# A gather kernel: eight of 180 superblocks fetched row by row with plain transfers from SyncE and ScalarE

## The reference

```
h = jnp.maximum(_layernorm(x, axis=-1), 0.0)
xs = h[src]
for i in range(4):
    mask = (edge_type == i)[:, None]
    msgs = msgs + jnp.where(mask, xs @ W[i] + b[i], 0.0)
out = x + jax.ops.segment_sum(msgs, dst, num_segments=N)
```

## Time and profile before

| | |
|---|---|
| timed runs, median of 3 | 2638.77 us (2616.4 to 2645.23) |
| profiled execution, span from its first to its last instruction | 2029.2 us |
| instructions in the profile | 24251 |
| mean granted clock of TensorE | 0.758 |
| DMA, mean over the span | 71 GB/s |

### The profile page before, as it was taken

How to read it: one execution, slowest core, us unless ns; L and a number is a source line. 1 busy time by engine, 2 the same in 40 slices (tenths; PEclk the granted TensorE clock), 3 DMA queues, 4 the chain that set the end, 5 groups by cost and what they waited for, 6 DMA issues and landing times.

```text
span 2029.2 us, 24251 instructions
## 1 busy us (share of the span) xinstructions
PE 1116.0 (55%) x5394; PEld 930.4 (46%) x5395; DVE 714.7 (35%) x1589; ACT 169.6 (8%) x565; POOL 1536.1 (76%) x1575
## 2 busy tenths in 40 slices
PE   6952545456564554654646556456555555554555
PEld 2322444344454444544535455445544444444554
DVE  6862223132332332433424334243322222232333
ACT  4530011010010100101001001010000000000000
POOL 7777777777777777777777777777777777777775
PEclk9985767776665776767878767787777777787788
DMA  9962221212122112211212121211312222212222
GB/s 305 328 206 54 51 52 50 53 49 52 51 50 52 50 49 52 51 51 49 50 52 50 50 52 50 51 50 50 104 51 70 51 51 52 69 51 52 69 52 59
DMA packets 94959, 144.09 MB, mean 71 GB/s; under 512 B 27065, under 2 KB 57267, under 8 KB 94947
## 3 DMA queue, kind: packets, MB, share of 16 engines
q0 software_dynamic: 50016, 102.53, 19.8%
q1 hardware_dynamic: 40537, 39.02, 5.8%
q10 hardware_dynamic: 4394, 2.40, 0.4%
HBM read 111.76 MB, written 32.09 MB: 71 GB/s over the span
## 4 chain that ended last, share of the span: by engine, by line
POOL 70%; issue 24%; PE 3%; DMA 1%; POOLq 1%; DVE 0%; ACT 0%; DVEq 0%; ACTq 0%; PEldq 0%
POOL messages L338 65%; POOL early_x L330 6%; PE ps_sum L710 2%; DMA messages<-message_table,row_stage 1%; PE ps_y L737 1%; PE ps_y L728 0%; POOLq L342 0%; POOLq L344 0%; DMA src_rows<-in_src 0%; PE ps_sum L746 0%; POOLq L345 0%; DVE onehot L593 0%; POOLq L246 0%; ACT row_stage L407 0%; DVE acc L585 0%
## 5 line engine op out<-in xcount | busy, mean ns | idle before, releaser
L338 POOL DMA_INDIRECT messages<-message_table,row_stage x1443 | 1420.5, 984 | 439.7 <-issue 437.9
L710 PE MATMUL ps_sum<-messages,onehot 128*128 128x128 f32 x4438 | 843.4, 370 | 852.9 <-DMA messages<-message_table,row_stage 769.7
L710 PEld LDWEIGHTS ps_sum<-messages,onehot 128*128 128x128 f32 x4438 | 791.0, 277 | 904.5 <-issue 890.5
L593 DVE SCALAR_TENSOR_TENSOR onehot<-node_iota,tile_base,dst_col 128x512 f32<-128x512 f32 x586 | 431.1, 749 | 1234.2 <-PE ps_sum L710 1147.0
L407 ACT COPY row_stage<-table_row 128x8 int32 (+2 forms) x181 | 35.7, 198 | 1602.5 <-PEq L715 1597.8
L330 POOL DMA_INDIRECT early_x<-in_x,src_col x120 | 113.5, 946 | 41.6 <-issue 39.4
L665 PE MATMUL ps_y<-w_sb,h_t 128*128 128x512 f32 x196 | 104.7, 626 | 4.6 <-DVE y L524 4.3
L737 PE MATMUL ps_y<-y 128*128 128x512 f32 x240 | 106.8, 598 | 0.0
L603 DVE SCALAR_TENSOR_TENSOR y<-key_iota,tile_base,key_col 128x1024 f32<-128x1024 f32 x60 | 75.9, 1285 | 35.5 <-PE ps_y L737 35.5
L585 DVE TENSOR_TENSOR acc<-acc,ps_sum x294 | 82.1, 279 | 2.3 <-PE ps_sum L710 2.1
L524 DVE TENSOR_TENSOR y<-ps_y,bias 128x512 f32<-128x512 f32 x98 | 66.9, 684 | 16.5 <-PE ps_y L665 11.4
(11 more groups left out here) (63 smaller groups left out, 147.5 us busy)
## 6 DMA issues: line engine op xcount, KB each, us to landing
message_table<-y SPq DMA_DIRECT2D x98, 256.0 KB
messages<-message_table,row_stage POOLq DMA_INDIRECT x1443
out<-acc SPq DMA_DIRECT2D x6, 896.0 KB
acc<-in_x SPq DMA_DIRECT2D x4, 896.0 KB, 7.5
early_x<-in_x,src_col POOLq DMA_INDIRECT x120
acc<-in_x ACTq DMA_DIRECT2D x2, 896.0 KB, 10.3
acc<-in_x SPq DMA_DIRECT2D x1, 832.0 KB, 6.9
src_rows<-in_src SPq DMA_DIRECT2D x1, 640.0 KB
```

Of the source, the lines that this page charges most:

```text
L338: pool.indirect_dma_start(messages[:, k, t, :], None, table_rows, bass.IndirectOffsetOnAxis(ap=row_stage[:, k, t:t + 1], axis=0)).then_inc ...
L593: nc.vector.scalar_tensor_tensor(out=onehot[:, a:z, :], in0=node_iota[:, :].unsqueeze(1).broadcast_to([P, z - a, P]), scalar=tile_base[:, ...
L710: ins = nc.tensor.matmul(ps_sum[:, bass.ds(q % 2, 1), 0:d], onehot[:, t, :], messages[:, k, t, :], start=(t == 0), stop=(t == tiles - 1))
```

## The change

Eight superblocks (`ROW_SBS`) leave GpSimd's list. For each of them SyncE fetches the 128 rows of each of 5 edge tiles (`SP_TILES`) and ScalarE those of the other 3, with one plain transfer for each row. A superblock's row numbers are first copied into one partition (`load_row_list`), then read 16 at a time into registers, and each register gives the row of one transfer (`fetch_rows`). The rows land in `row_messages`, two superblocks large, which uses the room of the lists of types and destinations (`pair_rows`); so the fetches wait until the first stage is over. When all rows of one have landed, each of the two engines counts a semaphore up, and TensorE waits for both. Seven of the row superblocks come after five rounds each (two of two with an early superblock behind, and one), the eighth ahead of the last round. SyncE's output stores stand behind all its row fetches.

The row numbers in the untransposed list are kept by a second multiply-add on VectorE (`table_rows_kept`). GpSimd's gathers are written out without a loop and read `table_row` directly; `row_stage` is gone, and GpSimd waits for the free slot itself. ScalarE's copies of the early sums move to VectorE. The order of superblocks changes accordingly in all engines, and the numbers in `order` with it.

```diff
+ROW_SBS = 8
+SP_TILES = 5
-    rounds = (full_sbs - EARLY_SBS) // SLOTS
+    rounds = (full_sbs - EARLY_SBS - ROW_SBS) // SLOTS
+    mixes = ROW_SBS - 1
+    mix_early = 2
+    mix_rounds = 2 * EARLY_ROUNDS + 1
+    def load_row_list(eng, n, rows, a, z, signal):
+        first = row_sb_id(n) * SB_TILES
+        eng.dma_start(rows[:, :].rearrange("o (t e) -> o t e", e=P),
+                      src_rows[first % P + a:first % P + z, first // P, :]).then_inc(signal, 16)
+        eng.wait_ge(signal, (n + 1) * 16)
+
+    def fetch_rows(eng, n, rows, row_at, t, signal):
+        regs = [eng.alloc_register(f"{eng.engine.name}_row{r}_{nc.next_id()}") for r in range(16)]
+        for q in range(P // 16):
+            eng.reg_load(regs, rows[0:1, bass.ds(row_at + q * 16, 16)])
+            for r in range(16):
+                p = q * 16 + r
+                row = eng.snap(regs[r], min_val=0, max_val=node_tiles * P * n_types - 1)
+                eng.dma_start(flat_row_messages[p:p + 1, bass.ds((t + (n % 2) * SB_TILES) * d, d)],
+                              table_rows[bass.ds(row, 1), :]).then_inc(signal, 16)
...
+            for n in range(ROW_SBS):
+                load_row_list(sp, n, sp_rows, 0, SP_TILES, sp_rows_loaded)
+                if n >= 2:
+                    sp.wait_ge(row_sb_used, n - 1)
+                with sp.Fori(0, SP_TILES) as t:
+                    fetch_rows(sp, n, sp_rows, t * P, t, sp_row_landed[n])
+                sp.wait_ge(sp_row_landed[n], SP_TILES * P * 16)
+                sp.sem_inc(sp_rows_gathered, 1)
+
             sp.wait_ge(store_after_ready, 1)
...
-            with pool.Fori(0, rounds) as i:
+            for i in range(rounds):
                 for k in range(SLOTS):
-                    pool.wait_ge(stage_ready, i * SLOTS + (k + 1))
-                    pool.sem_inc(slots_taken, 1)
-                    gather(k, SB_TILES)
-            pool.wait_ge(stage_ready, rounds * SLOTS + 1)
-            gather(0, last_tiles)
+                    gather(i, k)
+            gather(rounds, 0, last_tiles)
...
+            for n in range(ROW_SBS):
+                load_row_list(act, n, act_rows, SP_TILES, SB_TILES, act_rows_loaded)
+                make_early_h(n * mix_early)
+                if n >= 2:
+                    act.wait_ge(row_sb_used, n - 1)
+                fetch_rows(act, n, act_rows, 0, SP_TILES, act_row_landed[n])
+                if n < mixes:
+                    make_early_h(n * mix_early + 1)
+                with act.Fori(1, SB_TILES - SP_TILES) as t:
+                    fetch_rows(act, n, act_rows, t * P, t + SP_TILES, act_row_landed[n])
+                act.wait_ge(act_row_landed[n], (SB_TILES - SP_TILES) * P * 16)
+                act.sem_inc(act_rows_gathered, 1)
...
+                        dve.wait_ge(h_sums_done, p + 1)
+                        nc.vector.tensor_copy(h_sums[:, :, :], ps_y[:, 0, :].rearrange("f (t n) -> f t n", n=P)).then_inc(h_sums_ready, 1)
+                        nc.vector.tensor_copy(edge_counts[:, :], ps_y[:, 1, 0:P]).then_inc(h_sums_ready, 1)
...
+                    if rows_of is None:
+                        pe.wait_ge(gathered[k], needed)
+                    else:
+                        pe.wait_ge(sp_rows_gathered, needed)
+                        pe.wait_ge(act_rows_gathered, needed)
...
+                r = mix_early * EARLY_ROUNDS
+                table_round(s + r * SLOTS, n * mix_rounds + r)
+                row_superblock(s + mix_rounds * SLOTS, n)
```

More of the change, by code:

```diff
@@ L186, in gnn_program @@
     early_gathered = sem("early_gathered")
+    table_rows_kept = sem("table_rows_kept")
+    sp_rows_loaded = sem("sp_rows_loaded")
+    act_rows_loaded = sem("act_rows_loaded")
+    sp_row_landed = [sem(f"sp_row_landed{n}") for n in range(ROW_SBS)]
+    act_row_landed = [sem(f"act_row_landed{n}") for n in range(ROW_SBS)]
+    sp_rows_gathered = sem("sp_rows_gathered")
+    act_rows_gathered = sem("act_rows_gathered")
+    row_sb_used = sem("row_sb_used")
     e_stats_taken = sem("e_stats_taken")
@@ L334, in _, with table_sb_id, gather @@
                 pool.wait_ge(y_stored[k], 16 * node_tiles // Y_SLOTS)
-            def gather(k, tiles):
+            def table_sb_id(i, k):
+                if i < mixes * mix_rounds:
+                    return EARLY_SBS + i // mix_rounds * mix_ids + i % mix_rounds * SLOTS + k
+                i -= mixes * mix_rounds
+                return end_id + i * SLOTS + k + (1 if i >= end_rounds - 1 else 0)
+            pool.wait_ge(index_cols, groups + 1)
+            def gather(i, k, tiles=SB_TILES):
+                pool.wait_ge(slot_free[k], i + 1)
+                at = table_sb_id(i, k) * SB_TILES
                 for t in range(tiles):
@@ L487, in index_to_f32 @@
                                                    in1=type_rows[:, two, :], op0=ALU.mult, op1=ALU.add).then_inc(index_f_ready, 1)
+                    nc.vector.scalar_tensor_tensor(out=src_rows[:, two, :], in0=src_rows[:, two, :], scalar=float(n_types),
+                                                   in1=type_rows[:, two, :], op0=ALU.mult, op1=ALU.add).then_inc(table_rows_kept, 1)
                 elif part == 1:
@@ L617, in superblock, with run_with_early @@
                     dve.free_register(r)
[L619 to L620 removed]
+            def run_with_early(s, i):
                 superblock(s, SB_TILES)
@@ L699, in _, with superblock @@
             p_reg, early_count = counter(pe, "early_pair")
-            def superblock(s, k, tiles, needed):
+            def superblock(s, k, tiles, needed, free, rows_of=None):
                 lo, hi, regs = load_range(pe, s)
```

133 lines of the change are left out of this document (74 added, 59 removed).

## The result

The changed kernel takes 5716.3 us (median of 4 runs, 5710.6 to 5724.8), the kernel before beside it 2627.6 us (4 runs, 2614.0 to 2645.2). The ratio is 2.187, 95% interval 2.176 to 2.198. The prediction had the sign right and the size wrong: 3826 us was forecast, and 5716 lies outside the range too.

What follows compares the result with a forecast made beforehand. GpSimd's gathers bound the kernel before; after the change SyncE's row fetches would: 141 start + 2570 rows + 420 loads + 52 lists and waits + 33 last stretch = 3216 us, plus 609.6 outside the span = 3826 us; range 2530 to 5200.

Steps and rivals of the forecast that it cites:

- The bound of the kernel before: GpSimd's rate of one 128-row gather in 1.289 us, with GpSimd busy 76% of the 2029.2 us span.
- 82.5 us for 64 gathers: On GpSimd, 8 of 180 full superblocks leave: 64 gathers at 1.289 us each removed.
- SyncE's start at 141 us: SyncE's row fetches can start at about 141 us, after the table is stored and the list has landed.
- the register load of sixteen: On SyncE, one load per 16 rows, taken at 1.14 us; 320 with fused instruction and gaps make 420 us.
- the last stretch: Behind SyncE's last row: 27 us of TensorE's remaining work and 6 us for sums and stores.
- the mechanism: TensorE waits for SyncE at eight row superblocks, about 174 us each, frees no slots, and GpSimd stops.
- the row, forecast at 0.502 us without its load: On SyncE, each row costs 0.090 fused instruction, 0.08 dispatch and 0.332 transfer issue; 5120 rows make 2570 us.
- The prediction's estimate of 0.427 us: One transfer instruction on SyncE by the skill's 512 cycles at 1.2 GHz; would make the sum 4312 us.
- outside the span and fixed: The 609.6 us between timed median and profiled span were taken as outside the span and added to the sum.
- Rival 2: The 609.6 us belong to the work, so late SyncE gives 3216 us, or 2603 at lowest prices; chance 0.2.
- The chance of 0.12 on a dearer row: Rival: SyncE's rows cost more, up to 0.926 us of issue and 6867 us in all; over 4700, chance 0.12.
- Rival 3: Rows are hidden and GpSimd stays the bound: faster, 2556 or 2531 us; chance 0.18.

Runs made afterwards that it cites:

- e11: Kernel before, with only GpSimd's gathers reading offsets straight from the table's row and ScalarE's copies gone: 2030.0 us beside 2027.4, ratio 1.001.
- e10: Changed kernel with no row fetched at all, TensorE multiplying what the buffers hold: 1942.0 us beside 2027.4, ratio 0.958.
- e12: Changed kernel with all rows fetched, but GpSimd making one of eight gathers in its own superblocks: 4668.1 us beside 2027.4, ratio 2.303.
- e2: Changed kernel with row fetches written out for each tile, so each destination is constant and each row one piece: 4059.3 us, ratio 1.569.
- e0: Kernel before with only the register values bounded that SyncE waits against before output stores: 2595.1 us beside 2594.7, ratio 0.997.
- e17: The kernel of e12 once more in another group of runs: 4665.9 us beside 2028.0, ratio 2.299.
- e3: Changed kernel with only 16 of each tile's 128 rows fetched: 2583.0 us, ratio 0.999 to the kernel before.
- e15: The kernel of e3 once more in another group of runs: 2622.6 us, ratio 1.000.
- e4: On top of e2, ScalarE's three tiles of each row superblock not fetched: 3909.8 us, ratio 1.499.

## Why the prediction was wrong in size

**What held.** The bound of the kernel before, in a short group; the written-out gathers and ScalarE's copies at nothing (e11); 82.5 us for 64 gathers (85.3 in e10); SyncE's start at 141 us in a short group (139.9); the register load of sixteen, taken at 1.14 and measured at 0.973; the last stretch, roughly (33 us forecast, 44 in e12, 4663.8 less 4619.5); and the mechanism: TensorE waits eight times for SyncE, GpSimd stops for want of slots, GpSimd's gathers no longer set the time. That each wait is 370 us (2964.8 / 8) and not 174 comes of the dearer row, stalls included.

**First failed step: the row, forecast at 0.502 us without its load.** In e12, which has no stalls, the mean time from start to start is 0.120 for the fused instruction (0.130 was forecast with its gap), 0.065 for the MOVE (not in the sum) and 0.600 for the transfer with its gap (0.372 was forecast). Together 0.785: 0.283 us more on 5120 rows, 1449 us. The loads with their fused instructions came out at 348 us instead of 420. The order of instructions shows one register instruction ahead of a transfer, and I counted one; in the trace there are two. The kernel before has such a MOVE as well, ahead of 70 of its 98 table stores:

```profile
L280 SPq MOVE message_table<-y x70: 29/29/38, 36.0 to 132.6; - x70
```

The transfer I took from the nearest likeness of its addresses (0.332, 98 table stores). The row that was nearest in the shape of its pieces, many small ones into one partition, was the 0.926. With the same addresses of the source and the same bytes, 16 pieces took 0.547 and one piece 0.225 (e2). One reading of the rows was wrong, without much weight: 1.835 and 1.642 are the longest loads of two registers, but the first ones took 0.729 and 0.786.

By these the sum for the span is 140 + 4019 + 348 + 113 + 44 = 4664 us, where 4019 are the rows (5120 x 0.785) and 113 is what is left of the time from 140 to 4619.5 (52 forecast). Of these 113 us 91 go by in the branches that close 39 passes of the loops over tiles, 2.3 us each; the prediction had no term for them. My sum was 3216.

The prediction's estimate of 0.427 us rests on the 512 cycles that the Trainium skill, DMA: Bandwidth & Descriptors, gives for such an instruction on previous generations. No row here agrees: 0.225 for a whole row, 0.332 for a table store, 0.547 for a row in 16 pieces. The traces have no single figure per transfer; between the row in one piece and the row in 16 it differs by more than two.

**Second failed step: "outside the span and fixed".** A span was 1.8 to 2.3 us under its own execution's time in every run here. The 609.6 us were the difference between two kinds of executions: 107 us in the table stage and 462 in waits for slots, in e0. Rival 2 had them in the work, which is right. But it then let the late SyncE hide them, which is wrong: in the long groups SyncE is delayed too. Its rows start 130 us later (270 instead of 140) and lose 5120 x (1.055 - 0.875) = 922 us to stalls. 130 + 922 = 1052, and 5716.3 less the 4667 of e12 and e17 is 1049. Those two stand for the changed kernel in a short group, where it was not run itself.

**So the ledger** from 3826 to 5716: take the 609.6 out (3216), add 1448 for the row (1449) and the smaller terms, which cancel but for 1 us (4664), add 1052 for start and stalls (5716). The two errors of the second kind, +609.6 and -1052, partly cancelled. The 1448 us alone, with the 609.6 kept, would have given 5274, outside the range as well. The chance of 0.12 on a dearer row, "over 4700", named the right side, and the issue was indeed dearer (0.547, though not 0.926); it had neither the MOVE nor the stalls. That the time came out over 4700 is by that case's reasons only in part.

**Rival 3** was near to the truth in one place only: 1942 us in e10 shows what hiding would give. In the long groups even hidden rows give nothing (e3, e15).

**What stays open.** What makes a group long or short. In long groups the stalls stand beside GpSimd's gathers in six kernels, but gathers alone do not make them: in the table stage SyncE's fused, ALU and MOVE instructions run beside the same 120 early gathers in e0 and in e11, and the longest takes 2097 ns in e0, of a long group, and 94 in e11, of a short one. Whether the gathers are the cause in long groups or only the time at which another cause bites was not told apart, and nothing on record says what else ran on the chip. And why, in long groups, 64 gathers less gain nothing while 360 less gain 1.26 us each: e3 has not been run in a short group, nor e10 in a long one.

## What to carry to other kernels

An engine that fetches row by row pays for each row all instructions on its queue, not the transfer alone: read them off a trace (the order of instructions left one out here) and price each (here fused operation, MOVE, transfer, a sixteenth of a load: 0.85 us for 512 bytes, against 1.29 us for 128 rows by one gather). Before replacing an indirect gather divide: this one costs 0.010 us a row, so plain transfers can only help where their engine has fifty to ninety times as long to spare for each row (0.51 and 0.87 us). And where the profiled span and the timed median differ by far more than the 2 us that lie around a span, the two are different executions; find out which of the kernel's waits grew before a sum is made on either.

## What the runs showed of the hardware

- One transfer of a 512-byte row: 0.225 us of issue as one piece, 0.547 as 16 pieces of 32 bytes. With the destination offset in a register it was cut into 16, with a constant one it was not.
- A load of 16 registers takes 0.973 us on SyncE and 1.024 on ScalarE, against 0.537 for two.
- In long groups single instructions of SyncE, down to a semaphore increment of 17 ns, take up to 1.4 us (a fused instruction up to 1.8), and the time from start to start is 0.49 to 1.69 us instead of 0.28 to 0.87 while GpSimd issues gathers. In e12 and e17, both of short groups, the longest MOVE ahead of a row takes 38 ns and the longest fused instruction 87.
- From the branch that closes a loop pass around 128 row fetches to SyncE's next instruction it took 2.3 us (39 times, e12).
- ScalarE's fetching beside SyncE's cost SyncE little: with and without it a whole row takes 0.51 us while GpSimd does not gather (e2, e4). In e12 2315 of SyncE's issues lie over an issue of ScalarE for more than 100 ns, and their median is 547 ns, the same as of those that don't.
